# First layer of a four-layer network: the broadcast load of the decay sums as one transfer per piece

## The chip, the cores and the metric

One core of one Trainium2 chip runs the whole network in one launch. The metric is the device time of that launch in microseconds (us). The core's engines are PE (TensorE), DVE (VectorE), ACT (ScalarE), POOL (GpSimd) and SP (SyncE, which here issues transfers); 16 DMA engines move the data.

## The reference

Four layers, each with an attention-like half and a feed-forward half. The change is in the first layer's state-space half (2 sequences of 1024 tokens, 64 heads of 8 columns, state 128, chunks of 128 tokens):

```python
a = (dt * A).reshape(Bsz, nc, Q, H)
cum = jnp.cumsum(a, axis=2)
diff = cum[:, :, :, None, :] - cum[:, :, None, :, :]
Lmat = jnp.exp(jnp.where(tril, diff, -jnp.inf))
CB = jnp.einsum('bcihn,bcjhn->bcijh', Cc, Bc)
M = CB * Lmat * dtc[:, :, None, :, :]
Yd = jnp.einsum('bcijh,bcjhp->bcihp', M, xs_c)
states = jnp.einsum('bcqh,bcqhn,bcqhp->bchpn', wdec, Bc, xs_c)
```

The rest of that layer (a causal convolution, the recurrence over chunks, a gate and a norm, and eight experts with a shared feed-forward) and the three other layers are untouched.

## The kernel before, in words

Layer 0 works through 2048 tokens in four groups of 512 (`GROUP`), and each group in four chunks of 128 tokens (`NCH`). A group has two stages. In the first, PE does the input projections and the gate and up matmuls of twelve feed-forward units, with ACT's SiLU and DVE's products behind them. In the second, the chunk stage, the chunks' decay work goes on, with the down matmuls between it.

Within a chunk the kernel forms exact differences only inside blocks of 32 tokens (`BLK`, `NB` = 4 blocks). The tile `lc` holds the running sums of the decay within each block, tokens on partitions, 64 heads along. For the difference, each partition also needs the sums of all 32 tokens of its own block along its row. To get them, SP writes `lc` to DRAM (line 294, the tensor `l0_lc_rows`, one stretch of 2048 numbers per group, piece and chunk) and reads it back broadcast (line 304): partition p of `bc` receives the 32 x 16 numbers (2 KB) of block p // 32. A piece k is 16 heads; there are four pieces (`PIECES`) to a chunk, so 64 pieces in the layer. Each piece of `bc` is loaded by four transfers, one per block of 32 partitions, 256 in all.

The way of a piece, each step on its own engine and in the order of its program:

- SP waits (line 301) until ACT is done with the same piece of the chunk before (`e_ready`), since `bc` has one buffer per piece, and issues the transfers. Each adds 16 to `bc_landed[k]`.
- POOL waits for `bc_landed[k]` (line 665) and subtracts (line 666). POOL's program is: `differences(c+1)` (four pieces), `weigh(c+1)` (line 678: four products that make `rw`), the norm's power (line 658), `gate(c)` (line 687).
- ACT clamps (line 578) and takes the exponential (line 581) into the tile `e`, whose end is `e_ready`. ACT's program after chunk c is: pieces 0 to 2 of chunk c+1, the copy of chunk c's product `yd` (line 599), `place(c+1)` (line 546), piece 3 of chunk c+1, `square(c)` (line 587).
- DVE masks the piece (line 871, `near`), PE multiplies it with `xp`. The names `all_region_b` in the rows are `e` and `bc`.
- PE's program at the turn of a chunk is: `assemble(c)`, which waits for `yd`; then `from_before(c+1)`, one matmul from the state, then the matmuls of `rw`, which wait for POOL's line 678; then the four `near` pieces of chunk c+1 with down matmuls between them. `weigh` itself waits for DVE's `xdt` (line 834).

SP's program has, beside the pieces, the four writes of line 294 at the start of each group, and after the last group the loads of the next layer's weights (lines 308 and 310). Nothing is planned at run time: each engine runs its program in the order written.

Three transfers of layer 3 stand in the rows for comparison: line 1993 loads 128 rows of 192 B each, and lines 1999 and 2000 load three rows of 8 KB and three rows of 4 KB onto three partitions. Lines 1449 to 1452 issue bulk transfers, 128 rows on either side.

The helper `spread(ap, axis, n)` (line 116) inserts a dimension of n with stride 0.

Of the kernel before, what the change touches and what calls it, by code (L numbers as in the profile page):

```python
# [115 lines left out]
def spread(ap, axis, n):  # L116

    wide = ap.unsqueeze(axis)
    shape = list(wide.shape)
    shape[axis] = n  # L120
    return wide.broadcast_to(shape)


def layer0(nc, mem, ctx, io):

    sb, ps, sem = mem.scoped(ctx, "l0")
    BLK = 32
    NB = P // BLK
    PIECES, PH = 4, HEADS // 4
# [46 lines left out]
    e, bc = mem.l0_e, mem.l0_bc  # L176
# [6 lines left out]
    lc_d = nc.dram_tensor("l0_lc_rows", (TOKENS // GROUP, PIECES, GT, P * PH), F32).ap()  # L183
# [6 lines left out]
    NCH = GT  # L190
# [29 lines left out]
    bc_landed = [sem(f"l0_bc_landed{k}") for k in range(PIECES)]  # L220
# [52 lines left out]
    @block.sync  # L273
    def _(sp):
        x_d = io["x"].rearrange("(g t p) d -> g p t d", p=P, t=GT)
        sp.dma_start(x[:, 0:GT, :], x_d[0]).then_inc(w.gate_sem, 16)
        for g in range(1, TILES // GT):
            sp.dma_start(x[:, g * GT:(g + 1) * GT, :], x_d[g]).then_inc(mem.x_ready, 16)
        sp.dma_start(w.win, io["W_inT"].rearrange("(k p) n -> p k n", p=P)).then_inc(w.in_sem, 16)
        sp.dma_start(mem.l0_rows[:, :], io["l0_rows"].broadcast_to([P, N_L0_ROWS])).then_inc(mem.l0_row_ready, 16)  # L280
        sp.dma_start(mem.cols[:, :], io["cols"]).then_inc(mem.col_ready, 16)
        sp.dma_start(w.sh_gate_up, io["w_sh_gate_up"].rearrange("(k p) n -> p k n", p=P)).then_inc(w.ffn_sem, 16)
        sp.dma_start(w.gate_up,
                     io["w_gate_up"].rearrange("(ek p) f -> p ek f", p=P)).then_inc(w.ffn_sem, 16)
        sp.dma_start(w.down[:, 0:SHARED, :], io["w_sh_down"].rearrange("(e p) n -> p e n", p=P)).then_inc(w.ffn_sem, 16)
        sp.dma_start(w.down[:, SHARED:, :], io["w_down"].rearrange("(e p) n -> p e n", p=P)).then_inc(w.ffn_sem, 16)
        sp.dma_start(w.out, io["W_outT"].rearrange("(k p) n -> p k n", p=P)).then_inc(w.out_sem, 16)
        l1 = mem.l1
        sp.dma_start(l1.qkv, io["w_qkv"].rearrange("(k p) n -> p k n", p=P)).then_inc(l1.sem, 16)
        sp.dma_start(l1.out, io["w_attn_outT"].rearrange("(k p) n -> p k n", p=P)).then_inc(l1.sem, 16)  # L290
        for g in range(TOKENS // GROUP):
            sp.wait_ge(lc_ready.sem, lc_ready.done(g))
            for k in range(PIECES):
                sp.dma_start(lc_d[g, k].rearrange("c (p h) -> p c h", p=P), lc[:, :, k * PH:(k + 1) * PH]).then_inc(
                    lc_out, 16)
            sp.wait_ge(lc_out, 16 * PIECES * (g + 1))
            for c in range(NCH):
                n = g * NCH + c
                for k in range(PIECES):
                    if n > 0:  # L300
                        sp.wait_ge(e_ready.sem, e_ready.done(0, (n - 1) * PIECES + k))
                    for q in range(NB):
                        rows = lc_d[g, k, c].rearrange("(q n) -> q n", q=NB)[q:q + 1, :].broadcast_to([BLK, BLK * PH])
                        sp.dma_start(bc[q * BLK:(q + 1) * BLK, k, :, :].rearrange("p i h -> p (i h)"), rows).then_inc(
                            bc_landed[k], 16)
        last = TOKENS // GROUP - 1
        sp.wait_ge(gate_b.filled.sem, gate_b.filled.done(last, GATE_AT - 1))
        sp.dma_start(l1.w1, io["w1T"].rearrange("(k p) n -> p k n", p=P)).then_inc(l1.sem, 16)
        sp.wait_ge(up_b.filled.sem, up_b.filled.done(last, UP_AT + L0_UNITS - 1))
        sp.dma_start(l1.w2, io["w2T"].rearrange("(k p) n -> p k n", p=P)).then_inc(l1.sem, 16)  # L310
# [297 lines left out]
    def _(pool):  # L608
# [43 lines left out]
        with pool.Fori(0, BATCH) as b:  # L652
            with pool.Fori(0, HALVES) as half:
                g = b * HALVES + half
                def out_scale(c):

                    pool.wait_ge(ssq_ready.sem, ssq_ready.done(g, c))
                    nc.gpsimd.tensor_tensor(yr[:, 1:2], yr[:, 0:1], mem.neg_half[:, 0:1], ALU.pow).then_inc(
                        yr_ready.sem, 1)

                def differences(c):

                    for k in range(PIECES):
                        heads = slice(k * PH, (k + 1) * PH)
                        pool.wait_ge(bc_landed[k], 16 * NB * (g * NCH + c + 1))
                        nc.gpsimd.tensor_tensor(bc[:, k, :, :], bc[:, k, :, :], spread(lc[:, c, heads], 1, BLK),  # L666
                                                ALU.subtract).then_inc(dd_ready.sem, 1)

                def weigh(c):

                    pool.wait_ge(xs_ready.sem, xs_ready.done(g, c))
                    if c == 0:
                        pool.wait_ge(decay_ready.sem, decay_ready.done(g, 1))
                    else:
                        off_b.wait_filled(pool, g, 2 * c)
                    x3 = xdt[:, :].rearrange("p (h e) -> p h e", e=HEAD_P)
                    for i in range(4):
                        last = nc.gpsimd.tensor_tensor(rw[:, i, :].rearrange("p (h e) -> p h e", e=HEAD_P), x3,  # L678
                                                       spread(decay[:, i, c, :], 2, HEAD_P), ALU.mult)
                    last.then_inc(rw_ready.sem, 1)  # L680

                def gate(c):

                    if c == 0:
                        pool.wait_ge(z_ready.sem, z_ready.done(g))
                    pool.wait_ge(y_ready.sem, y_ready.done(g, c))
                    nc.gpsimd.tensor_tensor(yg[:, :, :], yg[:, :, :], zs[:, :, c * P:(c + 1) * P], ALU.mult).then_inc(
                        yg_ready.sem, 1)

                differences(0)  # L690
                weigh(0)
                for c in range(NCH):
                    if c + 1 < NCH:
                        differences(c + 1)
                        weigh(c + 1)
                    if c > 0:
                        out_scale(c - 1)
                    gate(c)
                out_scale(NCH - 1)
# [2157 lines left out]
```

## Time and profile before

| | |
|---|---|
| Median of 3 runs | 1718.62 us (1711.59 to 1721.74) |
| The profiled execution's own time | 1723.52 us |
| Its span, first to last instruction | 1721.8 us |
| Mean granted TensorE clock | 0.914 |
| PE busy | 1423.6 us (83%) |
| DVE busy | 926.6 us (54%) |
| ACT busy | 538.0 us (31%) |
| POOL busy | 350.5 us (20%) |
| Layer 0 | from 0 to about 735 us of the span |

The engines run beside each other, so their busy times don't add up to the span. A wait is idle time of an engine, put down to the one that released it. A granted clock of 1.00 is 2.4 GHz and 0.5 is 1.2 GHz; values between are means. A packet of the DMA view is what one DMA engine moves at a time; the share is of all 16 engines over the stretch shown.

### The profile page before, as it was taken

The numbers are of one execution on the slowest core, as the hardware profiler recorded it, in microseconds if no ns is written. First come the engines' busy times: TensorE is split into PE (matmuls) and PEld (weight loads), VectorE is DVE, ScalarE is ACT, GpSimd is POOL, SyncE is SP. The second block draws the span as 40 slices with busy tenths as digits, with TensorE's granted clock in tenths as the row PEclk, the third lists the DMA queues.
The fourth block names the chain that finished last, engine by engine and source line by source line (L and its number), as shares of the span: only waits on it lengthen the run. The fifth ranks groups of instructions, "written<-read, shape, count | busy, mean of one in ns | idle before, by whom it ended". The sixth has DMA issues, their size and how long they took to land. (4 is left out here: it accounts for less than half of the span.)

```text
span 1721.8 us, 22117 instructions
## 1 busy us (share of the span) xinstructions
PE 1423.6 (83%) x7388; PEld 861.4 (50%) x7388; DVE 926.6 (54%) x1942; ACT 538.0 (31%) x825; POOL 350.5 (20%) x311
## 2 busy tenths in 40 slices
PE   5987798769876987799999989888935398988986
PEld 2445445554444445556666654444533255644464
DVE  6366444735474537451320348898878444657434
ACT  1454054504451446122222223223301132233321
POOL 2145004600271027220030011000012600000034
PEclk9998799969997899899999989899965699999998
DMA  6110001100110013030000036000000200111113
GB/s 230 28 50 26 2 16 55 32 2 1 47 56 2 1 28 124 1 100 0 1 0 0 0 126 213 0 0 1 1 1 20 91 26 19 32 37 49 59 48 109
DMA packets 62074, 70.35 MB, mean 41 GB/s; under 512 B 16839, under 2 KB 48007, under 8 KB 61834
## 3 DMA queue, kind: packets, MB, share of 16 engines
q1 hardware_dynamic: 58892, 60.55, 11.2%
q0 software_dynamic: 3072, 8.39, 1.5%
q8 instruction: 63, 1.03, 0.2%
q14 instruction: 47, 0.38, 0.1%
HBM read 51.83 MB, written 17.08 MB: 40 GB/s over the span
## 5 line engine op out<-in xcount | busy, mean ns | idle before, releaser
L315 PE MATMUL l_b<-l_xnT,all_region_a 128*128 128x512 f32 x544 | 255.2, 620 | 15.9 <-ACTq L558 13.0
L315 PEld LDWEIGHTS l_b<-l_xnT,all_region_a 128*128 128x128 f32 x544 | 106.0, 199 | 143.2 <-issue 113.4
L666 POOL TENSOR_TENSOR all_region_b<-all_region_b,l_lc 128x512 f32<-128x512 f32 x64 | 93.2, 1472 | 326.0 <-DMA all_region_b<-l_lc_rows 325.7
L315 PE MATMUL l_b<-all_region_a,l_hT 128*128 128x256 f32 x384 | 114.1, 423 | 0.0
L1458 PE MATMUL l_banks<-l_xnT,mid_region_c 128*128 128x512 f32 (+1 forms) x192 | 96.1, 654 | 16.9 <-DVE l_xnT L1642 16.9
L855 DVE TENSOR_TENSOR l_hT<-all_region_b,l_b 128x512 f32<-128x512 f32 x48 | 33.0, 687 | 139.5 <-PE l_b L315 117.1
L2306 POOL TENSOR_TENSOR l_rstd<-l_moments,all_neg_half 128x4 f32<-128x4 f32 x20 | 20.8, 1038 | 337.6 <-DVE l_moments L2347 337.6
L315 PEld LDWEIGHTS l_b<-all_region_a,l_hT 128*128 128x128 f32 x384 | 72.7, 204 | 24.5 <-issue 15.3
L678 POOL TENSOR_TENSOR l_rw<-l_xdt,l_decay 128x512 f32<-128x512 f32 x64 | 72.6, 1165 | 35.3 <-DVE l_xdt L834 35.3
L315 PE MATMUL l_b<-all_region_b,l_xp 128*32 128x32 f32 x2048 | 31.6, 205 | 52.5 <-DVE all_region_b L871 52.5
L581 ACT ACTIVATE all_region_b<-all_region_b 128x512 f32<-128x512 f32 x64 | 69.4, 1084 | 17.9 <-PE l_b L315 14.3
L1458 PEld LDWEIGHTS l_banks<-l_xnT,mid_region_c 128*128 128x128 f32 (+1 forms) x192 | 37.7, 202 | 67.6 <-issue 49.4
L712 DVE SCALAR_TENSOR_TENSOR all_x<-l_b,l_comb,all_x 128x256 f32 x128 | 56.1, 479 | 22.8 <-PE l_b L315 16.2
L557 ACT ACTIVATE all_region_b<-l_b 128x512 f32<-128x512 f32 x48 | 28.7, 597 | 126.2 <-PE l_b L315 126.1
L871 DVE TENSOR_TENSOR all_region_b<-all_region_b,l_cbd 128x512 f32<-128x512 f32 x64 | 58.0, 907 | 18.6 <-ACT all_region_b L581 14.4
L315 PEld LDWEIGHTS l_b<-all_region_b,l_xp 128*32 128x32 f32 x2048 | 26.3, 118 | 77.3 <-DVE all_region_b L871 64.5
L1328 DVE TENSOR_TENSOR all_x<-all_x,l_banks 128x512 f32<-128x512 f32 x8 | 5.5, 688 | 100.1 <-PE l_banks L1071 100.1
L1071 PE MATMUL l_banks<-all_region_a,l_hT 128*128 128x256 f32 x256 | 56.3, 381 | 3.1 <-ACT l_hT L1192 3.1
L2026 PE MATMUL l_banks<-all_region_b,mid_region_c 128*128 128x256 f32 x256 | 56.1, 380 | 3.2 <-DVE mid_region_c L2583 3.2
L1071 PE MATMUL l_banks<-l_v,l_pT 128*128 128x256 f32 x256 | 57.6, 379 | 0.0
L800 DVE SCALAR_TENSOR_TENSOR l_xbc<-l_pre,all_cols,l_xbc 128x512 f32<-128x512 f32 x72 | 54.3, 754 | 5.5
L1071 PE MATMUL l_banks<-l_xnT,l_qT 128*128 128x512 f32 x128 | 57.2, 592 | 0.0
(393 smaller groups left out, 2763.7 us busy)
## 6 DMA issues: line engine op xcount, KB each, us to landing
all_region_b<-l_lc_rows SPq DMA_DIRECT2D x256, 64.0 KB, 2.0
l_slots_in<-mid_zeros SPq DMA_DIRECT2D x1, 4992.0 KB, 22.8
mid_vector_rows<-l_slots_in SPq DMA_DIRECT2D x39, 128.0 KB, 2.1
l_slots_out<-all_region_a SPq DMA_DIRECT2D x39, 128.0 KB, 1.7
all_region_a<-l_gate_up SPq DMA_DIRECT2D x1, 4096.0 KB, 14.8
all_x<-x SPq DMA_DIRECT2D x4, 512.0 KB, 5.4
all_region_a<-w_gate_up SPq DMA_DIRECT2D x1, 2048.0 KB, 17.5
all_region_a<-l_down SPq DMA_DIRECT2D x1, 2048.0 KB, 19.1
```

The costliest lines, as they stand in the source:

```text
L315: return nc.tensor.matmul(out, lhsT, rhs, start=start, stop=stop, **kw)
L557: nc.scalar.activation(sg[:, u % 2, :], bank[4][:, :], ACT.Silu).then_inc(silu_ready.sem, 1)
L581: nc.scalar.activation(e[:, k, :, :], part.rearrange("p i h -> p h i"), ACT.Exp, scale=-1.0).then_inc(e_ready.sem, 1)
L666: nc.gpsimd.tensor_tensor(bc[:, k, :, :], bc[:, k, :, :], spread(lc[:, c, heads], 1, BLK), ALU.subtract).then_inc(dd_ready.sem, 1)
L678: last = nc.gpsimd.tensor_tensor(rw[:, i, :].rearrange("p (h e) -> p h e", e=HEAD_P), x3, spread(decay[:, i, c, :], 2, HEAD_P), ALU.mult)
L712: last = nc.vector.scalar_tensor_tensor(out=xt, in0=bank[at][:, DIM * i:DIM * (i + 1)], scalar=scale, in1=xt, op0=ALU.mult, op1=ALU.add)
L800: nc.vector.scalar_tensor_tensor(out=xbc[:, j, :], in0=pre[:, j, i:i + GROUP], scalar=col("conv_w", j * CONV_K + i), in1=xbc[:, j, :], op0 ...
L855: nc.vector.tensor_tensor(hT[:, u, :], sg[:, u % 2, :], bank[5][:, :], ALU.mult).then_inc(hid_ready.sem, 1)
L871: nc.vector.tensor_tensor(e[:, k, :, :], e[:, k, :, :], spread(cbd[:, :], 1, PH), ALU.mult).then_inc(m_ready.sem, 1)
L1071: return nc.tensor.matmul(out, lhsT, rhs, start=start, stop=stop)
L1458: return nc.tensor.matmul(out, lhsT, rhs, start=start, stop=stop)
L2026: return nc.tensor.matmul(out, lhsT, rhs, start=start, stop=stop)
```

## The change

The loop over the four blocks goes. One transfer per piece takes the whole of `bc[:, k]` (128 partitions x 512 numbers) as its destination, and as its source a view of DRAM with three dimensions: 4 blocks at a stride of 512 numbers, 32 repeats at stride 0, 512 numbers at stride 1. POOL's wait counts 16 per piece in place of 64. The bytes, their source and their place are the same.

```diff
-                    for q in range(NB):
-                        rows = lc_d[g, k, c].rearrange("(q n) -> q n", q=NB)[q:q + 1, :].broadcast_to([BLK, BLK * PH])
-                        sp.dma_start(bc[q * BLK:(q + 1) * BLK, k, :, :].rearrange("p i h -> p (i h)"), rows).then_inc(
-                            bc_landed[k], 16)
+                    rows = spread(lc_d[g, k, c].rearrange("(q n) -> q n", q=NB), 1, BLK)
+                    part = bc[:, k, :, :].rearrange("p i h -> p (i h)")
+                    sp.dma_start(part, rows).then_inc(bc_landed[k], 16)
...
-                        pool.wait_ge(bc_landed[k], 16 * NB * (g * NCH + c + 1))
+                        pool.wait_ge(bc_landed[k], 16 * (g * NCH + c + 1))
```

## Rows read from the trace of the kernel before

**Rows 1.** Windows: busy us (count) by engine, granted clock, DMA share, GB/s.
```profile
105.00:121.00 16.00, 9.80 (x202) 6.50 (x200) 11.08 (x22) 14.33 (x18) 6.80 (x6) 1.00 0.33 94
121.00:142.00 21.00, 15.53 (x205) 10.36 (x195) 15.86 (x26) 13.67 (x19) 15.54 (x12) 0.92 0.25 70
```

**Rows 2.** Waits over the span: waiter, releaser, us in total, times, longest.
```profile
POOL all_region_b L666 <- DMA all_region_b<-l_lc_rows: 325.7, 28, 65.1
...
PE l_b L315 <- POOL l_rw L678: 3.6, 3, 1.3
...
PE l_b L315 <- ACT l_yd L599: 0.3, 1, 0.3
```

**Rows 3.** Source view of line 304, all 256 transfers: issue to landing.
```profile
DMA to landing us min/median/max: 1.8/2.0/3.4
```

**Rows 4.** SP's timeline, first pieces of group 0: start, duration, count.
```profile
75.28 7.30 SPq L304 DMA_DIRECT2D all_region_b<-l_lc_rows  x16
```

**Rows 5.** SP's timeline, pieces of chunk 1 of group 0.
```profile
108.33 1.69 SPq L304 DMA_DIRECT2D all_region_b<-l_lc_rows  x4
```

**Rows 6.** POOL's timeline, group 0: start, duration; in brackets the idle time before.
```profile
89.06 4.18 POOL L678 TENSOR_TENSOR l_rw<-l_xdt,l_decay 128x512 f32<-128x512 f32 x4 [3.52 <-DVE l_xdt L834]
111.78 1.61 POOL L666 TENSOR_TENSOR all_region_b<-all_region_b,l_lc 128x512 f32<-128x512 f32 x1 [18.54 <-DMA all_region_b<-l_lc_rows]
113.68 1.27 POOL L666 TENSOR_TENSOR all_region_b<-all_region_b,l_lc 128x512 f32<-128x512 f32 x1 [0.29 <-DMA all_region_b<-l_lc_rows]
116.23 1.27 POOL L666 TENSOR_TENSOR all_region_b<-all_region_b,l_lc 128x512 f32<-128x512 f32 x1 [1.28 <-DMA all_region_b<-l_lc_rows]
118.36 1.43 POOL L666 TENSOR_TENSOR all_region_b<-all_region_b,l_lc 128x512 f32<-128x512 f32 x1 [0.85 <-DMA all_region_b<-l_lc_rows]
119.75 4.62 POOL L678 TENSOR_TENSOR l_rw<-l_xdt,l_decay 128x512 f32<-128x512 f32 x4
124.33 1.26 POOL L687 TENSOR_TENSOR l_yg<-l_yg,l_zs 128x512 f32<-128x512 f32 x1
125.56 6.37 POOL L666 TENSOR_TENSOR all_region_b<-all_region_b,l_lc 128x512 f32<-128x512 f32 x4
134.28 4.62 POOL L678 TENSOR_TENSOR l_rw<-l_xdt,l_decay 128x512 f32<-128x512 f32 x4 [2.35 <-DVE l_xdt L834]
```

**Rows 7.** ACT's timeline, group 0: start, duration.
```profile
107.25 1.06 ACT L581 ACTIVATE all_region_b<-all_region_b 128x512 f32<-128x512 f32 x1
...
112.25 1.10 ACT L581 ACTIVATE all_region_b<-all_region_b 128x512 f32<-128x512 f32 x1
...
117.53 0.63 ACT L578 ACTIVATE all_region_b<-all_region_b 128x512 f32<-128x512 f32 x1 [0.65 <-POOL all_region_b L666]
...
119.24 0.60 ACT L599 ACTIVATE l_yd<-l_b 128x512 f32<-128x512 f32 x1
```

**Rows 8.** DVE's timeline, group 0: chunk 1's xdt.
```profile
117.06 0.68 DVE L834 TENSOR_TENSOR l_xdt<-l_b,l_dt 128x512 f32<-128x512 f32 x1
```

**Rows 9.** PE's timeline from 117 to 128 us, group 0.
```profile
122.16 1.02 PE L315 MATMUL l_b<-l_st,l_xbc 128*128 128x512 f32 x2
124.50 1.12 PE L315 MATMUL l_b<-l_rw,l_btok 128*128 128x512 f32 x2 [1.32 <-POOL l_rw L678]
```

**Rows 10.** DMA view, 75 to 84 us: packets; the queue's packets, MB, share.
```profile
DMA packets 768, 1.05 MB, mean 117 GB/s; under 512 B 256, under 2 KB 256, under 8 KB 768
...
q1 hardware_dynamic: 768, 1.05, 38.3%
```

**Rows 11.** DMA view of 1266 to 1272 us: 144 small packets of one transfer.
```profile
q1 hardware_dynamic: 144, 0.02, 2.1%
```

**Rows 12.** DMA view of 1293.3 to 1298 us: two transfers of three rows each.
```profile
DMA packets 12, 0.04 MB, mean 8 GB/s; under 512 B 6, under 2 KB 6, under 8 KB 9
```

**Rows 13.** DMA view of 1293.3 to 1294.94 us: the first of the two.
```profile
q1 hardware_dynamic: 4, 0.02, 6.0%
```

**Rows 14.** DMA view of 1040 to 1056 us: bulk loads.
```profile
DMA packets 5582, 6.10 MB, mean 382 GB/s; under 512 B 33, under 2 KB 5446, under 8 KB 5581
```

## The prediction, made blind

> **What bounds the kernel now.** I read the stage view first, then the waits, then the timelines of the engines at one turn of a chunk, then the DMA view. The change touches only layer 0, and in it the pieces of `bc`.
>
> The largest wait of the layer is POOL's for these pieces, 325.7 us [rows 2]. It misleads: most of it is POOL waiting, with nothing else to do, for a new group's sums. The first four pieces of a group are subtracted before `weigh(0)` at 89.06 [rows 6], and ACT takes the first exponential at 107.25 [rows 7]. What matters is who waits for POOL. PE does, three times, 3.6 us in all, for `rw`, and once 0.3 us for `yd` [rows 2]. Both are at one place: the turn from chunk 0 to chunk 1, where ACT, which had done nothing for a while, frees all four buffers in a row.
>
> Group 0 shows it. ACT ends the exponentials of chunk 0 between 108.31 and 113.35 [rows 7]. SP issues the first piece of chunk 1 at 108.33, four transfers in 1.69 us [rows 5]; over sixteen in a row one costs 7.30 / 16 = 0.456 us [rows 4], so a piece costs SP 1.83 us. POOL starts the four subtractions at 111.78, 113.68, 116.23 and 118.36, each after idle time that the DMA ended. Right behind the fourth comes `weigh(1)` at 119.75, whose last product ends at 124.37 [rows 6]. PE finishes the state's matmul and stands 1.32 us until 124.50 [rows 9]. So the chain is SP's issues, landing, POOL, PE. Three of the four groups wait there, one doesn't [rows 2]. At this turn POOL has no cushion: a fourth piece that is later by some time makes PE later by the same.
>
> **The change, part by part.**
>
> *Issues.* 256 become 64. A piece costs SP about 0.46 us in place of 1.83 [rows 4]. Nothing else is queued behind them that is urgent, so the gain is only in how early a piece starts.
>
> *Bytes and packets.* 16 transfers were 768 packets, 256 of them tiny [rows 10]: per transfer 32 packets of 2 KB and 16 tiny ones. The 128-row transfer of line 1993 was 144 packets [rows 11], 128 and 16. The two three-row transfers were 12 packets, six of them tiny [rows 12]: three and three each. I read the tiny ones as one completion for each DMA engine that takes part. So 32 and 128 rows went to 16 engines, three rows to three.
>
> *How many engines take the new transfer* is the step that decides. All of these had the same count of rows on both sides. The new one has 128 on the destination and an outermost count of 4 on the source. No row shows such a pair. From 16 to 3 the engines followed the outermost count, so I take four, each with one block: 32 packets of 2 KB one after another. The other end is 16 engines with eight packets each. The Trainium skill, "DMA: Bandwidth & Descriptors", Rules for kernel authors, says that an outermost dimension of size c under 16 confines a transfer to at most c engines, and "How many engines (k)" that it is the largest number up to 16 that divides both sides' outermost counts: four here. That rule speaks against this change; the same table's advice to coalesce many small transfers into one speaks for it. By the first the sum is the one below, by the second the first rival.
>
> *Price of a 2 KB packet.* From 75 to 84 us the queue took 38.3% of 16 engines, 0.383 x 16 x 9 = 55.2 us [rows 10]. The tiny packets cost 0.021 x 16 x 6 / 144 = 0.014 us each [rows 11], 3.6 us for 256. That leaves 51.6 / 512 = 0.101 us. Bulk transfers give the low end: 382 GB/s over 16 engines is 2 KB in 0.086 us [rows 14]. The high end is the three-row load: 0.060 x 16 x 1.64 = 1.57 us for 24 KB [rows 13], 0.131 us per 2 KB. I take 0.101, the same data read in the same way. A piece then occupies its four engines 32 x 0.101 = 3.2 us (2.75 to 4.2).
>
> *Landing.* A 64 KB transfer lands 2.0 us after issue [rows 3], of which two packets are 0.2; fixed are 1.8 us. POOL starts 0.2 us after landing: the fourth transfer is issued 1.27 us after the first, so at 109.60, and 2.0 us behind it is 111.6 against 111.78 [rows 5, 6]. I assume that all pieces go to the same four engines, so they queue. Issued at 108.33, the first lands at 113.3 and the others 3.2 us apart. POOL starts at 113.5, 116.7, 119.9 and 123.1, against 111.78, 113.68, 116.23 and 118.36 [rows 6]: later by 1.7, 3.0, 3.7 and 4.7 us.
>
> *Who waits next.* `weigh(1)` and with it `rw` are 4.7 us later, and PE's matmul goes from 124.50 to 129.2. On the other path ACT's clamp of piece 2 moves from 117.53 by 3.7 us, its exponential and `yd` (119.24) with it [rows 7], so `assemble(0)` and the state's matmul (122.16) [rows 9] end before 127: `rw` is the last. POOL's `gate(0)` (124.33) moves by 4.7 too; `square(0)` and the next chunk's pieces stand behind it. Chunk 2's pieces queue behind chunk 1's: the last lands by 122.9 + 12.8 = 135.7. POOL ended these four at 131.93, so it began the last at about 130.3 and would now want it at 135.0; 0.9 late. But `weigh(2)` stood 2.35 us for DVE's `xdt`, which moves with PE [rows 6], and that covers it. No new delay. Chunk 3's pieces are not freed before the turn is over, and have more room.
>
> *Cover that stays.* At the start of a group all four pieces go out at once: 75.28 + 1.8 + 12.8 = 89.9 for the last [rows 4], so `weigh(0)` moves from 89.06 [rows 6] to about 91.4. ACT and PE want this only from 105 on. That cover costs nothing and would hold at 4.2 us a piece.
>
> *Clock.* Where PE idles more, its granted clock may be lower: the mean fell from 1.00 to 0.92 between the two stretches [rows 1]. Another fall by 0.08 over the 15.5 us of PE's work in the second would be 1.4 us a group. I count 0.5, with 0 and 1.4 as ends.
>
> *Sum.* Four groups x 4.7 = 18.8, less 0.5 for the one group that had room, plus 2 for the clock: 20.3 us. Against the profiled execution that is 1723.5 + 20.3 = 1743.8. The median of the runs, 1718.6, lies 4.9 us under the profiled one; I give the number on the median: 1739. With 2.75 us a piece the fourth is late by 2.9 us: 11 us in all, 1730. With 4.2 us it is late by 8.8; chunk 2's last piece by 4.8 more, of which 2.35 are covered; the clock 1.4: (8.8 + 2.4 + 1.4) x 4 = 50, 1769.
>
> **The rivals.**
>
> *A. All 16 engines take it (not slower).* For: the destination has 128 rows, and every 128-row transfer here used 16. Then a piece lands 1.8 + 0.8 us after issue. The fourth, whose buffer is free at 113.35, is subtracted from about 116.2 and not 118.36. But `weigh(1)` also needs `xdt`, done at 117.74 [rows 8], so `rw` comes only 2.0 us earlier, and PE waited for it 3.6 us in all groups together and 0.3 for `yd` [rows 2]. The gain is at most 3.9 us: 1715. It decides from the point where the fourth piece lands before 118.2, which is any engine count that moves a piece in less than about 2 us.
>
> *B. Four engines, but other ones for each piece.* Then nothing queues: each piece lands 5.0 us after its own issue, the fourth at 113.35 + 5.0 + 0.2 = 118.5, against 118.36: no change, 1719. For: 16 engines stand idle most of this stretch. Against: the three-row loads don't tell which engines they took, and a fixed choice is simpler. "How many engines (k)" in the same page of the Trainium skill says that it is the lowest-numbered k, which is my case and not this one.
>
> *C. The three strides cost more than the engines.* If each packet is cut smaller, or four engines get in each other's way on the same rows, a piece costs more than 4.2 us. At 6 us it is late by 16 us a group, over 60 in all: over 1780. Nothing in the rows is for it but that 0.131 of the three rows was above the 0.101 of the many.
>
> **How the numbers follow.** No change can be told within 0.5%, 8.6 us. My forecast (four engines, in queue) has 0.72. Its low end, 11 us, is still over 0.5%, so all of it is slower. A has 0.16, B 0.05, C 0.05; 0.02 stay for what I haven't thought of. Slower: 0.72 + 0.05 = 0.77. Same: A and B, less a little for A with more gain than its bound by luck of the runs: 0.19. Faster: 0.04. The range goes from A's 1715, taken in nearly whole, to 1766, just under the far end of my own case; it leaves out C and the tails. My case's own range is 1730 to 1769.
>
> **What would show each step.** The tiny packets tell the engines: with four, a 128-row piece is 132 packets, with sixteen 144; over the 64 pieces 8448 or 9216. From issue to landing a lone piece takes about 5 us (A: 2.6), and queued ones up to 11. SP's line 304 is 64 issues of about 0.42 us. POOL's starts at the turn of group 0 are 3.2 us apart. PE waits for line 678 near 6 us in each group, about 22 us in all against 3.6. If POOL's starts are 1.7 us apart and that wait is gone, A holds. If POOL's wait grows and PE's does not, there was a cushion that I missed, and my number is wrong though the engines are right.

## The result, and the profile after

The changed kernel took 1728.11 us against 1718.62, medians of nine runs each; the ratio is 1.0053, with a 95% interval of 1.0029 to 1.0077. That is 9.1 us (5.0 to 13.2) where 20.3 were forecast: the sign was right and so were the four engines with their queue, but the size was over twice too large. Beside the last experiments the same kernel came out at 1.0026 (1.0002 to 1.0051), 4.5 us: the intervals overlap, and the loss is real but no better known than that.

The page of the kernel after (PE's and the packets' lines):

```profile
span 1726.3 us, 21925 instructions
...
PE 1430.7 (83%) x7388; PEld 864.3 (50%) x7388; DVE 922.7 (53%) x1942; ACT 538.1 (31%) x825; POOL 346.8 (20%) x311
...
DMA packets 58232, 70.33 MB, mean 41 GB/s; under 512 B 12998, under 2 KB 44166, under 8 KB 57993
```

Packets fell from 62074 to 58232, and those under 512 B by 3841. Sixteen completions on each of 256 transfers are 4096, four on each of 64 are 256: 3840 fewer. So by the completions four DMA engines take each piece, as forecast.

The source view of line 304, and the DMA view of ten us at the start of group 0, where four pieces stand in the queue:

```profile
L304 SPq DMA_DIRECT2D all_region_b<-l_lc_rows x64: 509/510/734, 76.7 to 689.8; - x64
```

```profile
DMA packets 494, 0.99 MB, mean 99 GB/s; under 512 B 12, under 2 KB 12, under 8 KB 494
...
q1 hardware_dynamic: 494, 0.99, 25.9%
```

The queue's share is 25.9% of 16 engines: the times of its packets add up to 4.1 engines' full time, and there are no packets but its own. With four pieces waiting, that fits four engines that never rest and twelve that stand idle. The 482 packets of 2 KB (494 less the 12 completions) took 10 us, so one of four engines takes one every 0.083 us. An issue costs SP 0.51 us (median) in place of 0.42.

POOL's timeline at the turn from chunk 0 to chunk 1 of group 0, to be laid beside [rows 6]; then ACT's [rows 7] and PE's [rows 9]:

```profile
115.06 1.27 POOL L665 TENSOR_TENSOR all_region_b<-all_region_b,l_lc 128x512 f32<-128x512 f32 x1 [20.25 <-DMA all_region_b<-l_lc_rows]
117.67 1.30 POOL L665 TENSOR_TENSOR all_region_b<-all_region_b,l_lc 128x512 f32<-128x512 f32 x1 [1.34 <-DMA all_region_b<-l_lc_rows]
120.27 1.28 POOL L665 TENSOR_TENSOR all_region_b<-all_region_b,l_lc 128x512 f32<-128x512 f32 x1 [1.30 <-DMA all_region_b<-l_lc_rows]
122.89 1.27 POOL L665 TENSOR_TENSOR all_region_b<-all_region_b,l_lc 128x512 f32<-128x512 f32 x1 [1.34 <-DMA all_region_b<-l_lc_rows]
124.11 4.63 POOL L677 TENSOR_TENSOR l_rw<-l_xdt,l_decay 128x512 f32<-128x512 f32 x4
```

```profile
108.68 1.06 ACT L580 ACTIVATE all_region_b<-all_region_b 128x512 f32<-128x512 f32 x1
...
121.57 0.63 ACT L577 ACTIVATE all_region_b<-all_region_b 128x512 f32<-128x512 f32 x1 [0.78 <-POOL all_region_b L665]
...
123.27 0.58 ACT L598 ACTIVATE l_yd<-l_b 128x512 f32<-128x512 f32 x1
```

```profile
123.98 1.08 PE L314 MATMUL l_b<-l_yd,l_turn 128*32 128x128 f32 x32 [0.32 <-ACT l_yd L598]
...
125.98 1.02 PE L314 MATMUL l_b<-l_st,l_xbc 128*128 128x512 f32 x2
128.87 1.12 PE L314 MATMUL l_b<-l_rw,l_btok 128*128 128x512 f32 x2 [1.86 <-POOL l_rw L677]
```

All times here are 1.4 us later than before, since ACT's first exponential of the group begins at 108.68 and not 107.25 (of the change only chunk 0's pieces lie ahead of it, and in the fourteen traces of this record it begins anywhere from 106.5 to 108.9, with one transfer or with four). From that exponential on, the subtractions begin after 6.4, 9.0, 11.6 and 14.2 us; before after 4.5, 6.4, 9.0 and 11.1. They are 2.6 us apart, each behind idle time that the DMA ended. The fourth is 3.1 us late, `rw` ends 20.1 us after the exponential in place of 17.1, PE waits 1.86 us for it, and before that 0.3 for `yd`, which is 2.6 us late (14.6 in place of 12.0). In the other three groups `rw` ends 2.6, 2.8 and 2.8 us later than before: 11.1 us for the four.

The waits of the span, to be laid beside [rows 2]:

```profile
POOL all_region_b L665 <- DMA all_region_b<-l_lc_rows: 355.4, 32, 67.1
...
POOL l_rw L677 <- DVE l_xdt L833: 23.6, 8, 3.0
...
PE l_b L314 <- POOL l_rw L677: 5.6, 3, 1.9
...
PE l_b L314 <- ACT l_yd L598: 4.9, 4, 2.4
```

PE's wait for `rw` grew only from 3.6 to 5.6 us, but that for `yd` from 0.3 to 4.9. Together that is 6.6 us more, while PE begins the products of `rw` 2.9, 2.6, 3.5 and 2.8 us later after the exponential. The rest stands in neither row. In group 0 PE came to its last piece of chunk 0 already 2.0 us later. Its clock had been at 1.2 GHz from 0.9 to 7.7 us after the exponential, where before it was at 2.4; that the one made the other isn't shown. In group 2 it was at 1.2 GHz from 14.4 to 21.2 us, so that its work on `yd` and the state took 5.7 us in place of 3.0, and `rw` was there when it came. Windows of group 0 before and after, and of group 2 after (columns as in [rows 1]):

```profile
108.20:114.90 6.70, 4.38 (x84) 2.85 (x84) 5.71 (x9) 6.34 (x9) 2.83 (x2) 1.00 0.43 118
```

```profile
109.60:116.35 6.75, 5.20 (x77) 2.93 (x78) 4.16 (x7) 4.92 (x7) 1.27 (x1) 0.50 0.20 73
485.20:491.80 6.60, 5.86 (x43) 4.26 (x44) 1.42 (x6) 4.83 (x8) 6.00 (x6) 0.50 0.26 96
```

How much of the 11.1 us reaches the end? Windows of the chunk stage, from the first exponential to about the start of the last `yg` of each group (columns as in [rows 1]: length, busy us of PE, PEld, DVE, ACT, POOL, granted clock, DMA), before and then after:

```profile
107.20:185.80 78.60, 59.45 (x873) 41.28 (x873) 53.75 (x101) 37.77 (x51) 37.91 (x30) 0.91 0.15 42
285.40:363.90 78.50, 60.41 (x873) 42.31 (x873) 53.18 (x101) 37.81 (x50) 38.56 (x30) 0.89 0.15 42
465.60:544.00 78.40, 59.38 (x873) 40.97 (x873) 53.35 (x101) 37.71 (x50) 38.29 (x30) 0.91 0.15 42
643.50:722.00 78.50, 61.31 (x873) 43.13 (x873) 52.89 (x100) 37.85 (x51) 38.62 (x30) 0.87 0.22 68
```

```profile
108.70:188.10 79.40, 62.28 (x873) 42.84 (x873) 52.44 (x100) 37.82 (x50) 36.96 (x30) 0.85 0.11 41
287.70:368.80 81.10, 63.04 (x873) 43.13 (x873) 52.74 (x101) 37.72 (x50) 37.01 (x30) 0.85 0.11 40
470.70:552.80 82.10, 62.06 (x873) 43.35 (x873) 52.29 (x101) 37.80 (x50) 36.91 (x30) 0.88 0.11 40
652.40:730.40 78.00, 58.95 (x873) 40.16 (x873) 51.53 (x100) 37.78 (x50) 36.95 (x30) 0.91 0.21 69
```

The four stages are 314.0 us long before and 320.6 after. In the second trace of the changed kernel (the slowest of its twelve executions, 1739.4 us against a median of 1725.4) they were 328.5. So a delay of `rw` of 11.1 us came out as 6.6 in one execution and, being 11.4, as 14.5 in another. What differs between these two is the clock, which goes back and forth between 2.4 and 1.2 GHz within a stage. The mean granted clock was 0.85, 0.85, 0.88 and 0.91 in the first, and 0.83, 0.85, 0.81 and 0.84 in the second. Group 3 after has the clock at 0.91, and is shorter (78.0) than before (78.5, at 0.87) although its turn was 2.8 us late.

### The profile page after: what moved, and what is told of

Same layout as the page of the kernel before. It is cut to its first block and busy times, and to the rows that moved or that the text cites. A ratio compares the mean times of both kernels' runs of the same rounds, so it can differ in the third digit from the quotient of the medians.

```text
span 1726.3 us, 21925 instructions
## 1 busy us (share of the span) xinstructions
PE 1430.7 (83%) x7388; PEld 864.3 (50%) x7388; DVE 922.7 (53%) x1942; ACT 538.1 (31%) x825; POOL 346.8 (20%) x311
## 2 busy tenths in 40 slices
DMA packets 58232, 70.33 MB, mean 41 GB/s; under 512 B 12998, under 2 KB 44166, under 8 KB 57993
## 3 DMA queue, kind: packets, MB, share of 16 engines
q1 hardware_dynamic: 55052, 60.53, 10.5%
## 5 line engine op out<-in xcount | busy, mean ns | idle before, releaser
L665 POOL TENSOR_TENSOR all_region_b<-all_region_b,l_lc 128x512 f32<-128x512 f32 x64 | 87.2, 1378 | 355.4 <-DMA all_region_b<-l_lc_rows 355.4
L1457 PE MATMUL l_banks<-l_xnT,mid_region_c 128*128 128x512 f32 (+1 forms) x192 | 96.3, 655 | 16.9 <-DVE l_xnT L1641 16.9
L870 DVE TENSOR_TENSOR all_region_b<-all_region_b,l_cbd 128x512 f32<-128x512 f32 x64 | 56.4, 882 | 18.6 <-ACT all_region_b L580 14.4
```

The lines of the kernel that those rows point to most:

```text
L870: nc.vector.tensor_tensor(e[:, k, :, :], e[:, k, :, :], spread(cbd[:, :], 1, PH), ALU.mult).then_inc(m_ready.sem, 1)
L1457: return nc.tensor.matmul(out, lhsT, rhs, start=start, stop=stop)
```

## The experiments

All ratios are to the kernel before, on the same chip, with a 95% interval. Times "at the turn" are counted from ACT's first exponential of the group.

**Sixteen engines for the single transfer.** After the sums are written, one more transfer per group lays each 2 KB block down four times, and the piece's source has an outermost count of 16.

```diff
+    COPIES = 4
+    lc_e = nc.dram_tensor("l0_lc_copies", (TOKENS // GROUP, PIECES * GT * NB, COPIES, BLK * PH), F32).ap()
...
+            sp.dma_start(lc_e[g], spread(lc_d[g].rearrange("k c (q n) -> (k c q) n", q=NB), 1, COPIES)).then_inc(
+                lc_out, 16)
...
+                    at = (k * GT + c) * NB
+                    rows = spread(lc_e[g, at:at + NB].rearrange("q j n -> (q j) n"), 1, BLK // COPIES)
```

> One transfer per piece as in the change, but its source has an outermost count of 16: after the write of the sums one more transfer per group lays each block's 2 KB down four times, and each piece is read as 16 rows of 2 KB, each repeated 8 times. Engines theory (the change is slower since a piece runs on 4 DMA engines, 2.6 us each, and pieces queue on them at the turn from chunk 0 to chunk 1): 128 + 16 packets per piece, POOL's fourth subtraction of chunk 1 starts about 9.5 us after ACT's first exponential of the group (before 10.7 to 11.1, after 13.7 to 14.2), PE's waits for rw and yd at the turn vanish, time 0.997 to 1.000 of before. Rival (one large transfer with three strides has a longer fixed latency, whatever the engines): the fourth subtraction stays near 13 us, time about 1.005.

Measured: 1.0004 (0.9982 to 1.0025), just over the range expected. The source view of its piece loads, the DMA view of 108 to 124 us, and POOL's timeline at the first turn:

```profile
L310 SPq DMA_DIRECT2D all_region_b<-l_lc_copies x64: 514/515/600, 80.1 to 688.0; - x64
...
DMA to landing us min/median/max: 2.9/3.2/4.7
```

```profile
DMA packets 1010, 1.86 MB, mean 116 GB/s; under 512 B 112, under 2 KB 112, under 8 KB 1008
...
q1 hardware_dynamic: 1008, 1.84, 36.0%
```

```profile
112.35 2.96 POOL L671 TENSOR_TENSOR all_region_b<-all_region_b,l_lc 128x512 f32<-128x512 f32 x2 [18.42 <-DMA all_region_b<-l_lc_copies]
115.63 1.59 POOL L671 TENSOR_TENSOR all_region_b<-all_region_b,l_lc 128x512 f32<-128x512 f32 x1 [0.32 <-DMA all_region_b<-l_lc_copies]
117.94 1.28 POOL L671 TENSOR_TENSOR all_region_b<-all_region_b,l_lc 128x512 f32<-128x512 f32 x1 [0.71 <-DMA all_region_b<-l_lc_copies]
119.58 4.63 POOL L683 TENSOR_TENSOR l_rw<-l_xdt,l_decay 128x512 f32<-128x512 f32 x4 [0.37 <-DVE l_xdt L839]
```

A piece lands in 3.2 us. The fourth subtraction begins 10.0, 10.4, 9.4 and 9.4 us after the exponential, and PE's waits for `rw` and `yd` are gone from the list. The rival, a fixed cost of one large transfer with three strides, wanted the fourth subtraction near 13 us, and is ruled out by this; the time, 1.0004, fits that the loss is gone. The fourth subtractions are 4 us ahead of before in the four groups together, but `rw` ends only 0.4 us earlier in all (16.3, 16.3, 17.7 and 17.7 us): in three of the groups POOL now waits for DVE's `xdt`, which itself ends at 11.5 to 12.9 us where it was 10.3 to 10.5 before. So hardly any gain is left. Rival A of the forecast had named this bound, and put it too high. Why `xdt` is later I haven't traced.

**Eight engines.** The same with two copies.

> The same with two copies: outermost count 8. Engines theory: 128 + 8 packets per piece, 16 packets or 1.3 us on each engine, less than the 1.7 us at which ACT frees the buffers, so nothing queues; fourth subtraction about 10.2 us after the first exponential, time 0.998 to 1.001 of before. Fixed latency rival: 13 us, 1.005.

Measured: 0.9988 (0.9961 to 1.0014), as expected; the fourth subtraction begins at 10.2, 11.6, 10.2 and 10.5 us. Eight engines are enough: at 16 packets of 0.081 us a piece takes them an estimated 1.3 us, less than the 1.7 us at which ACT frees the buffers.

**Two engines.** Two transfers per piece, each of 64 partitions.

```diff
+                    for i in range(2):
+                        rows = spread(lc_d[g, k, c].rearrange("(q n) -> q n", q=NB)[2 * i:2 * i + 2, :], 1, BLK)
```

> Two transfers per piece, 64 partitions each, outermost source count 2. Engines theory, the same two engines for both: 128 + 4 packets per piece, a piece takes 5.2 us, the fourth subtraction of chunk 1 starts about 24.6 us after the first exponential, 13.7 us later than before in each group, and chunk 2 adds some 4 to 6; time 1.035 to 1.047 of before. If each transfer gets other engines: a piece 2.6 us, about 1.005. Fixed latency rival: about as after, 1.005.

Measured: 1.0275 (1.0241 to 1.0310), 47 us, less than the 1.035 to 1.047 expected. POOL's timeline at the first turn (the exponential begins at 107.61), and PE's waits:

```profile
116.75 1.27 POOL L666 TENSOR_TENSOR all_region_b<-all_region_b,l_lc 128x512 f32<-128x512 f32 x1 [12.02 <-DMA all_region_b<-l_lc_rows]
121.97 1.26 POOL L666 TENSOR_TENSOR all_region_b<-all_region_b,l_lc 128x512 f32<-128x512 f32 x1 [3.95 <-DMA all_region_b<-l_lc_rows]
127.18 1.26 POOL L666 TENSOR_TENSOR all_region_b<-all_region_b,l_lc 128x512 f32<-128x512 f32 x1 [3.95 <-DMA all_region_b<-l_lc_rows]
132.40 1.27 POOL L666 TENSOR_TENSOR all_region_b<-all_region_b,l_lc 128x512 f32<-128x512 f32 x1 [3.96 <-DMA all_region_b<-l_lc_rows]
133.62 4.17 POOL L678 TENSOR_TENSOR l_rw<-l_xdt,l_decay 128x512 f32<-128x512 f32 x4
```

```profile
PE l_b L315 <- ACT l_yd L599: 40.2, 4, 10.7
...
PE l_b L315 <- POOL l_rw L678: 27.9, 10, 4.0
```

The subtractions are 5.2 us apart and the fourth begins 24.8 us after the exponential, as expected to 0.2 us. So both transfers share two engines, and the price is 64 packets of 0.081 us. Here the delay carries through whole: `rw` is 13.1 us late and the stages are 13.0 us longer than before. What did not come is the further delay that I had counted for chunk 2, and that is the miss in the time.

**One transfer in chunk 1 alone, and in all others but chunk 1.**

```diff
+                    if c == 1:
+                        sp.dma_start(part, rows).then_inc(bc_landed[k], 16)
+                    else:
+                        for q in range(NB):
...
+                        pool.wait_ge(bc_landed[k], 16 * (g * 13 + (4, 5, 9, 13)[c]))
```

The second kernel has `c != 1` and counts to match.

> Only chunk 1 of each group is loaded by one transfer per piece, the others by four as before. If the whole loss is at the turn from chunk 0 to chunk 1: time as after, 1.003 to 1.008 of before, the fourth subtraction at 14 us. If the loss is spread over the chunks, or is no loss of this load at all: 1.000 to 1.002.

> Only chunk 1 of each group is loaded by four transfers per piece, chunks 0, 2 and 3 by one. If the loss is all at the turn from chunk 0 to chunk 1: 0.999 to 1.001 of before, and the fourth subtraction of chunk 1 at 10.7 to 11.1 us after the first exponential. If it is spread over the chunks: about 1.004.

Measured: 1.0081 (1.0056 to 1.0107) for chunk 1 alone, at the top of the range expected, 1.0004 (0.9977 to 1.0031) for all but chunk 1. The whole loss is at this one turn; 48 of the 64 pieces can go on four engines at no cost that shows, and with four transfers in chunk 1 its fourth subtraction begins at 10.8 to 11.2 us, as before. In the first kernel it begins at 15.0, 14.9, 14.5 and 15.0 us and not at 14. Chunk 2's transfers, which use all sixteen engines, go out from 9 us on and move beside the fourth piece; that they hold it up is the likely cause, argued and not tested.

**Two buffers.** Odd chunks have a buffer of their own, so chunk 1's pieces land before the turn. It lies where the next layer's first weights were, which are now loaded at the end of the layer.

```diff
+    bcs = [mem.l0_bc, mem.region_b[:, 0:2048].rearrange("p (a i h) -> p a i h", a=PIECES, h=PH)]
...
+                    bc = bcs[c % 2]
+                    if n > 1:
+                        sp.wait_ge(e_ready.sem, e_ready.done(0, (n - 2) * PIECES + k))
```

> One transfer per piece as in the change, but even and odd chunks have a buffer each (the odd one where the next layer's first weights lay, which are loaded at the end of the layer instead), so chunk 1's pieces land before the turn. Engines and queue theory: PE's waits for rw (line 678 of before) and yd at the turn are gone, rw is bounded by DVE's xdt and ends 15.2 us after the first exponential in place of 17.1 (before) and 19.9 (after); time 0.996 to 0.999 of before. A rival by which the single transfer costs something elsewhere (SP, contention, next layer's load): above 1.002.

> The same two buffers with four transfers per piece. Engines and queue theory: the same time as with one transfer within 0.2%, since nothing waits for landing any more. Rival: it keeps the 0.5% lead that before has over after.

Measured: 1.0029 (1.0007 to 1.0052) with one transfer, 1.0023 (0.9998 to 1.0048) with four. The two are alike within their intervals, as they should be once nothing waits for landing. `rw` ends at 14.5 to 15.8 us and PE waits for neither `rw` nor `yd`. But both are a little above before, where 0.996 to 0.999 was expected: that was a miss. The move of the weights' load and a lower clock (four stages of 316.0 and 317.8 us against 314.0) are candidates, and I haven't parted them.

**The order on ACT and POOL.** What PE waits for at the turn are `rw` and `yd`, which in their engines' programs stand behind pieces that nobody needs yet. Here POOL does `weigh` after two of the four subtractions, and ACT does the copy `yd` and `place` before the last two exponentials; the loads are those of the change.

```diff
-                        for k in range(PIECES - 1):
+                        for k in range(2):
                             exps(c + 1, k)
...
-                        exps(c + 1, PIECES - 1)
+                        for k in range(2, PIECES):
+                            exps(c + 1, k)
...
-                        differences(c + 1)
+                        differences(c + 1, 0, 2)
                         weigh(c + 1)
+                        differences(c + 1, 2)
```

> The loads as in the change; POOL does weigh(c+1) after two of the four subtractions, and ACT copies yd and places xdt before the last two exponentials of the next chunk. What is late in after at the turn is the third and fourth piece; if it costs only by standing ahead of rw and yd on POOL and ACT, then PE's waits for both vanish, rw ends about 16.5 us after the first exponential (after two subtractions at 6.2 and 8.8, weigh from 10.5 on), and the time is 0.997 to 1.001 of before. If PE needs the late pieces themselves soon after: 1.003 to 1.006 as after.

Measured: 0.9920 (0.9894 to 0.9947), better than the 0.997 to 1.001 expected: 14 us faster than before. PE waits for neither `rw` nor `yd`, and `rw` ends at 14.6 to 16.9 us although the fourth subtraction begins only at 16.3 to 18.5.

**The changed kernel again, and each half of that order alone.**

> The changed kernel itself, once more beside the three that follow. Engines and queue theory: rw ends 2.5 to 3 us later than before at each of four turns, 10 to 12 us in all, 1.004 to 1.007 of before. A rival by which the 0.5% was luck of the granted clock: below 1.002.

> The change with ACT's half of the new order alone (yd and place before the last two exponentials). PE's waits for yd go, but rw still ends at 19.9 us after the first exponential, behind the fourth subtraction, and PE waits for it 3 to 4 us at each turn: 1.003 to 1.006 of before, as after. If yd was what PE waited for: 0.996 or less.

> The change with POOL's half alone (weigh after two subtractions). The third subtraction then starts at about 15 us after the first exponential, ACT's third exponential ends at about 18, and yd, which stands behind it on ACT, comes at 18 in place of 14.5: PE waits 5 to 6 us for yd at each turn, 1.004 to 1.010 of before. If rw alone held PE: 0.996 or less.

Measured: 1.0026 (1.0002 to 1.0051) for the changed kernel, which is under the range expected and overlaps with it. With ACT's half alone it was 1.0073 (1.0045 to 1.0100), with POOL's half alone 1.0123 (1.0092 to 1.0154), each a little over its expected range. PE's largest wait for the turn, in the first and in the second:

```profile
PE l_b L314 <- POOL l_rw L678: 17.8, 4, 4.7
```

```profile
PE l_b L314 <- ACT l_yd L598: 30.7, 9, 5.5
```

With ACT's half, `yd` is early (11.7 to 12.2 us), and PE simply stands 4.5 us per turn before `rw`. With POOL's, `rw` is early and PE stands before `yd`, which begins 19.1 to 20.3 us after the exponential. Each half uncovers the other's wait. Only both together remove it. In the changed kernel, too, the 4.9 us that PE stood before `yd` hid a part of its wait for `rw`.

**Both halves with the four transfers of before.**

> Both halves of the new order, with the four transfers of before. If the order takes the late pieces off the way of PE, the number of engines no longer matters: 0.990 to 0.994 of before, within 0.2% of the same order with one transfer. If landing still counts: 0.985 to 0.988, the 0.5% better.

Measured: 0.9897 (0.9873 to 0.9922), the fastest kernel here, about 18 us faster than before. POOL's timeline at the first turn, and two of its four stages:

```profile
118.50 4.63 POOL L679 TENSOR_TENSOR l_rw<-l_xdt,l_decay 128x512 f32<-128x512 f32 x4 [3.34 <-DVE l_xdt L836]
123.09 2.95 POOL L667 TENSOR_TENSOR all_region_b<-all_region_b,l_lc 128x512 f32<-128x512 f32 x2
```

```profile
107.60:184.10 76.50, 60.57 (x873) 42.18 (x873) 51.03 (x100) 37.60 (x50) 37.61 (x30) 0.89 0.15 43
284.90:356.20 71.30, 55.52 (x873) 38.83 (x873) 51.68 (x101) 37.69 (x51) 37.84 (x30) 0.95 0.16 46
```

`weigh(1)` begins as soon as DVE has `xdt`. The four stages are 297.8 us long; with the single transfer they were 297.5, against 314.0 before. In this order one transfer or four makes no difference that the traces show: `rw` ends at 14.6 to 16.9 us with one and at 15.3 to 16.2 with four. The two ratios, 0.9920 and 0.9897, are from different batches and their intervals overlap, so 0.2% between them is neither shown nor excluded. The gain is far more than the 3.9 us that PE had waited at the first turn: the later turns became shorter too (from the copy `yd` of chunk 1 to that of chunk 2, 18.6 us in three groups and 20.2 in one; before 19.7 to 21.5), and the clock was granted more.

## Why the prediction was right or wrong

*How many engines.* Right: four, and the same four each time. The completions count the four (3840 fewer), pieces 2.6 us apart say that they are the same ones, and with outermost counts of 2, 8 and 16 the completions and the starts of the subtractions follow the count. The rule of the Trainium skill ("DMA: Bandwidth & Descriptors", "How many engines (k)"), the largest number up to 16 that divides both outermost counts, held for 2, 4, 8 and 16. Rivals A and B fell with it: A, since the fourth subtraction came 3.1 us later and not 2.2 earlier; B, since the starts are 2.6 us apart where ACT frees the buffers 1.7 us apart. C wanted more than 4.2 us a piece; it is 2.6.

*The price of a 2 KB packet.* This is the step that failed: the term was 0.101 us and measured 0.081 (2.6 us for 32). I took a mean over a stretch in which sixteen engines worked on overlapping 64 KB transfers, and the nearest row was not the row with the right load. By the same working (share x 16 x window, less 0.014 us for each completion) the sixteen engines of the first experiment come to 0.101 again (0.360 x 16 x 16 us, 896 packets), and the four of the changed kernel to 0.086 (0.259 x 16 x 10 us, 482 packets). Why packets take longer with sixteen engines at work isn't shown. The rest, 0.086 against 0.081, is that a packet's recorded time overlaps the next one's a little, so the share comes out over four engines. Even my low end, 0.086 [rows 14], was too high; it was a rate of sixteen engines whose packets were nearly all under 2 KB (5446 of 5582), read as the price of one of 2 KB. The high end, 0.131 from three packets of 8 KB [rows 13], had nothing to do with a stream. With 2.6 us a piece my own working gives 108.33 + 1.8 + 10.4 + 0.2 = 120.7, 2.4 us late in place of 4.7. The measured kernel, 1728, is also faster than the near end of my own case, 1730.

*The fixed part.* The fourth subtraction was 3.1 us late, 0.7 more than that. The first began 5.29 us after its issue, 2.7 beside its own 2.6 of packets, where I had 2.0.

*Who waits next.* `rw` was 2.8 us late on average (4.7 forecast). That PE would stand before it about 22 us in all was wrong: 5.6, and 4.9 for `yd`. My own rows had it: I let `yd` move by 3.7 us and PE's state matmul with it, and then still counted all of the 4.7 as PE's wait for `rw`. With both moved the wait in group 0 grows by 1.0 us, from 1.3 to 2.3, and not to 6; it measured 1.9. `yd` itself was 2.6, 1.0, 2.0 and 2.4 us late, less than the 3.7 I gave it, because each of ACT's exponentials waits for its own piece and the pieces were 2.6 and not 3.2 us apart. So PE was held in two places, one after the other, and the later of the two, `rw`, still says how late the turn is: 11.1 us in all. This error changed what I said would be seen, not the sum.

*The clock.* I added 0.5 us a group. Over the 56 chunk stages of the kernels traced (before, after and the twelve others), a least-squares fit of the stage's length gives about 1.2 us for each us that the last `near` of chunk 1 is late, and about 0.4 us for each us at the lower clock after it, with about 0.9 us left over. A stage has 7 to 38 us at the lower clock, and the two traces of the same changed kernel differ by 8 us in their stages. At the size of this delay the term can't be told from scatter: over the twelve executions of the second batch the mean clock was 0.910 with the change and 0.909 before. It gave back part of the delay in one trace and added to it in the other. With a delay of 13 us a turn, on two engines, the mean clock did fall, to 0.9005 against 0.9096.

*The sum.* 11.1 us at the turns against 18.3 forecast, and no further delay in chunk 2, as forecast; 9.1 (5.0 to 13.2) measured at the end in one batch and 4.5 (0.3 to 8.8) in the other. So whether all of the 11.1 us reaches the end stays open. The cover at the group's start held: `weigh(0)` moved from 89.06 to 90.63 where I had 91.4, and with four transfers in chunk 1 alone, and chunk 0 on four engines, no loss was left.

## What to carry to other kernels

One transfer in place of several saves the issuing engine time, but the outermost counts of its two sides set how many DMA engines carry it: with 4 here, a quarter of the engines did all of the work and pieces queued behind each other. What that costs is read where the consumer has no cushion, here at the pieces of one chunk in four; at the others it cost nothing that shows. Take the price of a packet from a row with as many engines at work as the new transfer will have: by the same working sixteen at once took 0.101 us a packet here, four 0.086. When an engine's program puts work that nobody needs yet ahead of what the bottleneck waits for, mend the order first and both halves of it: that gave 0.8% with one transfer and 1.0% with four, and left no difference between the two that these runs can tell.

## What the runs showed that I had not expected

An issue of the new transfer costs SP 0.51 us, with eight engines 0.58 and with sixteen 0.515, against 0.42 for the 64 KB ones. Four engines carry 99 GB/s and two 49, so an engine that streamed 2 KB packets did 25 GB/s whether three others worked beside it or one. When a queue was behind, SP's own issue grew: in the kernel on two engines its median was 2.5 us and its longest 4.5. And pieces that come 4 us earlier in all (sixteen engines) need not shorten the kernel: `weigh(1)` then waited for DVE's `xdt` in three groups of four, and `rw` ended only 0.4 us earlier in all.
